# A decoder layer on one core: the last two output projections in front of context products 4 to 6, and the weight splits behind them

## What is computed

```
x = layernorm(x + attn(x))            # 32 heads of 32, then @ attn_ow + attn_ob
q1 = (clip(round(x / s1 + z1), 0, 255) - z1) * s1
q2 = (clip(round(ctx / s2 + z2), 0, 255) - z2) * s2      # ctx: 2 x 1024 x 1024
x = layernorm(x + q1 @ q2)
logits = x @ W_router.T               # 8 experts, the best two weighted
hw = (x @ A.T) * combine              # 8 experts of rank 16
x = layernorm(x + x @ W_base.T + b_base + hw @ B * 2)
```

## Time and profile before

| | before |
|---|---|
| median of 3 runs | 758.9 us (757.3 to 759.88) |
| profiled execution, time | 757.49 us |
| profiled execution, span | 755.7 us |
| PE busy | 720.2 us, 95% |
| DVE busy | 461.1 us, 61% |
| ACT busy | 427.0 us, 57% |
| POOL busy | 246.6 us, 33% |
| mean granted TensorE clock | 0.981 |

### The profile page before, as it was taken

How to read it: one execution, slowest core, us unless ns; L and a number is a source line. 1 busy time by engine, 2 the same in 40 slices (tenths; PEclk the granted TensorE clock), 3 DMA queues, 4 the chain that set the end, 5 groups by cost and what they waited for, 6 DMA issues and landing times.

```text
span 755.7 us, 11772 instructions
## 1 busy us (share of the span) xinstructions
PE 720.2 (95%) x3512; PEld 535.6 (71%) x3512; DVE 461.1 (61%) x831; ACT 427.0 (57%) x919; POOL 246.6 (33%) x189
## 2 busy tenths in 40 slices
PE   7989999999999999999999997996999987999996
PEld 5767768668668668668668664664766755888884
DVE  5867557557557567467567463416564699666564
ACT  5458668668668668668668576524555564221111
POOL 6260330240240240240140176636535275031111
PEclk9999999999999999999999997998999998999999
DMA  9665436436435435435433646526642153113101
GB/s 298 193 169 180 113 85 194 111 85 195 109 90 188 110 89 188 112 88 189 111 88 109 175 135 216 174 71 197 221 139 85 62 190 112 57 58 110 56 29 56
DMA packets 56020, 98.97 MB, mean 131 GB/s; under 512 B 11184, under 2 KB 21680, under 8 KB 55088
## 3 DMA queue, kind: packets, MB, share of 16 engines
q1 hardware_dynamic: 55696, 98.13, 42.4%
q10 hardware_dynamic: 288, 0.39, 0.2%
HBM read 56.41 MB, written 16.65 MB: 97 GB/s over the span
## 4 chain that ended last, share of the span: by engine, by line
PE 71%; issue 13%; DVE 5%; POOL 5%; DMA 2%; ACT 2%; SPq 2%; POOLq 0%; DVEq 0%; ACTq 0%
PE bank L451 43%; PE bank L574 8%; PE bank L588 8%; PE bank L544 7%; PE bank L699 2%; POOL xb L1158 2%; SPq L236 2%; PE bank L502 1%; POOL mv L1137 1%; DVE st L1415 1%; POOL big_lo L1150 1%; DMA cx_raw<-ctx_scratch 1%; ACT quant L901 0%; ACT x1s L897 0%; DMA xres<-in_x 0%
## 5 line engine op out<-in xcount | busy, mean ns | idle before, releaser
L840 ACT ACTIVATE probs<-bank 128x512 f32<-128x512 f32 x256 | 153.1, 598 | 134.2 <-PE bank L574 131.6
L1336 DVE TENSOR_REDUCE m_col<-bank 128x1 f32<-128x512 f32 x256 | 172.7, 687 | 86.8 <-PE bank L544 86.2
L845 ACT ACTIVATE bank<-bank,m_col 128x512 f32<-128x512 f32 x256 | 169.5, 662 | 14.1 <-DVE m_col L1336 13.2
L451 PE MATMUL bank<-big_hi,w_hi 128*128 128x512 f32 x384 | 157.4, 410 | 5.5 <-DVE big_lo L1233 5.5
L451 PE MATMUL bank<-big_lo,w_hi 128*128 128x512 f32 x384 | 153.0, 399 | 0.0
L451 PE MATMUL bank<-big_hi,w_lo 128*128 128x512 f32 x384 | 151.6, 395 | 0.0
L574 PE MATMUL bank<-qp,kp 98*128 98x512 f32 x256 | 102.9, 402 | 2.2 <-DMA qp<-m_row 2.2
L544 PE MATMUL bank<-kp,qp 96*128 96x512 f32 x256 | 102.7, 401 | 2.0 <-ACT bank L845 2.0
L1087 POOL TENSOR_SCALAR c_raw<-c_raw,sc 128x1024 f32<-128x1024 f32 x16 | 19.3, 1204 | 255.8 <-DMA c_raw<-in_ctx 250.9
L451 PEld LDWEIGHTS bank<-big_hi,w_hi 128*128 128x128 f32 x384 | 73.4, 191 | 24.9 <-DVE big_lo L1233 6.0
L451 PEld LDWEIGHTS bank<-big_hi,w_lo 128*128 128x128 f32 x384 | 73.1, 190 | 17.2
(11 more groups left out here) (140 smaller groups left out, 1021.5 us busy)
## 6 DMA issues: line engine op xcount, KB each, us to landing
w_raw<-in_wqkv SPq DMA_DIRECT2D x7, 1536.0 KB, 7.0
c_raw<-in_ctx SPq DMA_DIRECT2D x16, 512.0 KB, 4.0
qp<-q_hi SPq DMA_DIRECT2D x128, 64.0 KB, 2.0
kp<-k_hi SPq DMA_DIRECT2D x124, 64.0 KB, 2.0
big_raw<-in_xT SPq DMA_DIRECT2D x16, 256.0 KB, 5.4
qp<-q_lo SPq DMA_DIRECT2D x64, 64.0 KB, 2.0
c_scratch<-c_q SPq DMA_DIRECT2D x16, 256.0 KB, 2.2
r_all<-r_scratch SPq DMA_DIRECT2D x64, 64.0 KB, 2.0
```

Of the source, the lines that this page charges most:

```text
L451: mm = nc.tensor.matmul(dst, lhs[a], rhs[b], start=(k == 0 and n == 0) if first is None else False, stop=(k == last_k and n == 2))
L840: nc.scalar.activation(probs[:, j, t, :], bank(ST0 + i % 2), ACT.Exp).then_inc(sem["exp_ok"], 1)
L845: nc.scalar.activation(bank(MAX[n % 3]), bank(MAX[n % 3]), ACT.Exp, bias=m_col[:, n:n + 1], accum_out=l_col[:, 1 - par, n:n + 1]).then_inc ...
L1336: nc.vector.reduce_max(m_col[:, n:n + 1], bank(MAX[n % 3]), AX, negate=True).then_inc(sem["rowmax"], 1)
```

## The change

On TensorE both halves of tile 7's output projection come directly behind tile 6's; after them `transpose_c1(5)`, product 4, `transpose_c1(6)`, `transpose_x2(0)`, product 5, `hidden(0)`, product 6. The other engines' lists follow: rounding and splits of base half 0 stand directly behind tile 6's quantisation, and product 4's work behind them. On GpSimd both corrections and both bias sums move back, on SP the store of x2 tile 4 moves behind the loads of base half 1. The instructions are the same in number and shape.

```diff
@@ sync
             sp.dma_start(bb_sb[:, :], bb.rearrange("(a n) -> a n", a=1).to_broadcast([P, H])).then_inc(sem["bt_in"], 16)
-            store_x2(4)
             sp.wait_ge(sem["cx_split"], NT // 2)
...
                 sp.dma_start(big_raw[:, k, S:2 * S], wbT[k * P:(k + 1) * P, S:2 * S]).then_inc(big_in[1][k], 16)
+            store_x2(4)
             store_x2(5)
@@ tensor
             for n in (6, 7):
                 for h in range(2):
                     out_project(n, h)
-                transpose_c1(n - 1)
-                context_product(n - 2)
+            transpose_c1(5)
+            context_product(4)
+            transpose_c1(6)
             transpose_x2(0, 0, 0)
+            context_product(5)
+            hidden(0)
             context_product(6)
-            hidden(0)
             last_step(0, 0, 0, True)
@@ scalar
             normalise_x2(3)
-            copy_c1T(5)
-            scale_product(4)
             normalise_x1(6)
-            centre_c1(6)
-            normalise_x2(4)
             for k in range(KT):
                 round_wb(0, k)
+            copy_c1T(5)
+            centre_c1(6)
+            scale_product(4)
             copy_c1T(6)
-            scale_product(5)
             copy_x2T(0, first_x2_banks)
             normalise_x1(7)
+            scale_product(5)
+            centre_c1(7)
+            normalise_x2(4)
+            exp_logits(0)
             scale_product(6)
-            exp_logits(0)
-            centre_c1(7)
-            for k in range(4):
-                round_wb(1, k)
             normalise_x2(5)
-            for k in range(4, KT):
+            for k in range(KT):
                 round_wb(1, k)
             normalise_x2(6)
@@ gpsimd
             rstd1(6)
-            add_correction(6)
-            rstd2(4)
             for k in range(1, KT, 2):
                 split_wb(0, k)
             rstd1(7)
+            add_correction(6)
+            rstd2(4)
+            add_correction(7)
+            rstd2(5)
+            for k in range(1, KT, 2):
+                split_wb(1, k)
+            rstd2(6)
             pool.wait_ge(sem["bt_in"], 32)
             add_bias(0, 0, 0)
-            rstd2(5)
-            add_correction(7)
-            split_wb(1, 1)
-            split_wb(1, 3)
-            rstd2(6)
-            split_wb(1, 5)
-            split_wb(1, 7)
             add_bias(1, 1, 0)
@@ vector
             first_mean(6)
-            add_product(4)
-            row_correction(5)
             quantise(6)
-            product_stats(4)
-            second_mean(4)
             for k in range(0, KT, 2):
                 split_wb(0, k)
             residual_sum(7)
+            first_mean(7)
+            add_product(4)
+            row_correction(5)
+            split_x2T(0, 0)
+            quantise(7)
+            product_stats(4)
+            second_mean(4)
             add_product(5)
             row_correction(6)
-            first_mean(7)
-            split_x2T(0, 0)
+            route(0)
             product_stats(5)
-            quantise(7)
             second_mean(5)
-            route(0)
+            split_wb(1, 0)
+            split_wb(1, 2)
             add_product(6)
             row_correction(7)
-            split_wb(1, 0)
-            split_wb(1, 2)
-            product_stats(6)
             split_wb(1, 4)
             split_wb(1, 6)
+            product_stats(6)
             second_mean(6)
```

## The result

The change takes 765.07 us (median of 4 runs, 764.28 to 766.52) against 758.1 us of the kernel before (4 runs, 757.0 to 759.88): ratio 1.0092, 95% interval 1.0065 to 1.0119. The forecast was 766.1 us, in a range from 758.5 to 769.5. A second set of 4 runs of the same kernel, given further down, came out at 766.96 us, ratio 1.0123.

What follows compares the result with a forecast made beforehand. VectorE's chain up to the split of the transposed expert weights, as late as TensorE's, was taken to decide; +6.0 + 1.7 - 0.5 = +7.2 us gave a median of 766.1 us, range 762 to 769.5 (758.5 to 769.5 with variants).

Steps and rivals of the forecast that it cites:

- Front part and SP's queue: TensorE up to the first base half: 2.4 us ahead; the late x2 store costs 0.7 us, nothing in the sum.
- Middle: VectorE's chain to the second base half's split: TensorE starts that half 1.8 us earlier, after waiting 4.2 us.
- Back part, +6.0: VectorE before the split of hw: bias sums on GpSimd hold bt_hi and bt_lo; split comes 6.0 us later.
- the difference of two counts, 5.7: Split of hw: forward count of the new order against the same count over the old order, 5.7 us later.
- the plain count of 7.3: VectorE's chain counted forward to the split of hw, 644.55 against 637.23 in the trace of before: 7.3 us late.
- the count of the old order: The same forward count over the old order, to the split of hw: 638.8, 1.6 us later than the trace.
- Clock, +1.7: TensorE after its 8 us wait for the split of hw: half clock costs 1.7 us, bounds 0 and 2.6.
- hw(1), -0.5: TensorE's wait of 0.5 us for hw(1) goes, since VectorE has that 0.5 by then: -0.5 us.
- Sum: Whole kernel: +6.0 + 1.7 - 0.5 = +7.2 us, median 766.1 us.
- The faster rival: TensorE's new density pays as VectorE's chain reaches the hw split before the second base half ends: 755 us, chance 0.10.
- The same: Rival: bias sums do not hold up the bt pair, so 4.7 us go: +2.5, 761.4 us, chance 0.12.
- The signs named for a wrong forecast: transpose_c1(7) starting before 638 us, or bt_lo done before the second add_bias.

Runs made afterwards that it cites:

- The first experiment: The change, with GpSimd waiting for bt_ok so both bias sums come behind the bt pair: 762.04 us, ratio to the kernel before 1.0052.
- four strips ahead: The change, with ScalarE rounding four strips of the second weight half in front of normalise_x2(5) instead of behind it: 765.21 us, ratio 1.0082.
- the filler experiment: The change, with 28 matmuls nobody reads added on TensorE behind the second base half of tile 0: 764.75 us, ratio 1.0096.
- the combination of all moves: The change's TensorE order, with strips, weight splits, the bt pair and scale_product(7) moved on the other engines: 758.2 us, ratio to the kernel before 0.9994.
- bt off VectorE: The combination of all moves, with bt_hi on ScalarE, bt_lo on GpSimd, and copy_x2T(1) and two VectorE splits moved ahead: 755.71 us, ratio 0.9969.
- its variant with a late sum: The kernel before, with add_bias(0) moved to just in front of add_bias(1), all else in the old order: 759.22 us, ratio 1.0015.

## Why the prediction was right

The count on VectorE can be laid beside the trace step by step, in us from the mark (the prediction counted from 590.6):

| step | counted | measured |
|---|---|---|
| VectorE's splits of the first half end | 13.0 | 13.2 |
| product 4's matmuls end on TensorE | 14.8 | 14.8 |
| add_product(4) ends | 20.1 | 20.3 |
| first base half starts on TensorE | 25.5 | 25.6 |
| add_product(5) ends | 28.9 | 29.0 |
| routing ends | 31.9 | 32.0 |
| second base half starts on TensorE | 36.8 | 37.1 |
| bt_lo ends | 53.4 | 52.9 |
| split of hw ends | 53.95 | 53.4 |

- **Front part and SP's queue.** Right. TensorE has two waits of 0.3 us in place of 0.76 and 2.14; `transpose_x2(1)` starts 31.7 us from the mark, as counted for the late store, and the 0.7 us disappear in the wait behind it.
- **Middle.** Right: the wait in front of the second base half is 4.23 us (4.2 counted). What I left out is that this wait too is followed by low clock: eight matmuls from 626.13 took 3.46 us in place of 1.8. It costs nothing, since TensorE waits for VectorE afterwards.
- **Back part, +6.0.** It measured +6.54. The first experiment shows the meeting of the sums with the bt pair as the cause of 4.05 of them, where 4.7 were counted; the other 2.5 come from what stands ahead on VectorE's list, and four strips ahead took back 2.1 us. The size was set a little low: I took a value near the difference of two counts, 5.7, where the truth lies between it and the plain count of 7.3. The plain count came within 0.5 us of the place; the count of the old order is what erred.
- **Clock, +1.7.** It measured 1.99, 2.12 in the second execution of the change, and 1.9 in the filler experiment. The clock was at half until some 4.3 us after the restart in place of 3.4, since it was still at 0.50 in 644:646 and at 0.81 in 646:648.
- **hw(1), -0.5.** This term was a misreading. The row has one wait of 0.5 us somewhere behind 640 us, and it is not that of hw(1) but that of tile 7's hw, near the end. It is still there in the change. First the kernel before, then the change, from TensorE's timelines:

```profile
741.83 0.33 PE L752 MATMUL bank<-ident,hw 128*128 128x128 f32 x1 [0.53 <-DVE hw L1512]
748.66 0.33 PE L752 MATMUL bank<-ident,hw 128*128 128x128 f32 x1 [0.52 <-DVE hw L1510]
```

  Before, `transpose_hw` of tile 1 starts 1.07 us behind the start of `transpose_x2(2)`, in the change 0.87: there were 0.2 us to gain at hw(1), most of the 0.28 that came out.
- **Sum.** +7.2 forecast, +8.25 from the mark (6.54 + 1.99 - 0.28), +6.8 by the spans of the two profiled executions, +7.0 by the medians, and +8.8 by those of the second set. All three terms were off to the same side, 1.05 us together. That 766.1 still lies so near 765.07 is luck: the part ahead of the mark moves by 2 us between two executions of one kernel.

The faster rival needed VectorE to be 9 us ahead of the count; it is 0.5 ahead. *The same* is out by the change's own rows, where the bt pair takes 2.70 and 3.24 us beside the sums. Its price for them, 4.7 us, was near the 4.05 that the first experiment took off; but with the sums out of bt's way the end is 4.9 us behind before, not 2.5, since the rest of the delay was larger than forecast and the sums and the clock take their toll one step later. The signs named for a wrong forecast did not appear: `transpose_c1(7)` starts at 642.49, and `bt_lo` ends at 641.90, behind both sums.

What my later expectations got wrong is worth as much. They treated the split of hw(0) as the only gate. Behind it ScalarE's copies of x2T and c1T come late as well, and the same sums, moved, hold x2T of tile 1 and through it hw(1). And in the combination of all moves I added up gains of single experiments, which overlap, where VectorE's filled time should have been counted.

## What to carry to other kernels

Denser work on the busiest engine was worth nothing here until the engine that feeds it arrived earlier too: count that engine's list forward to the instruction that gates the next part. When long two-input instructions of GpSimd are moved, look at what VectorE does at that very moment, and then at what it does one step later; the cost depends on the neighbour: one sum moved back cost 1.55 us at the end in the old order, and two sums beside the bt pair cost 3.4 in the new one. For differences of 1 to 2 us in 760, compare traces from a common mark rather than whole times. And look up where a wait stands before it enters a sum: a total over a stretch does not say to which tile it belongs.

## What the runs showed of the hardware

- The length of a wait alone doesn't tell whether the clock falls behind it. Behind 3.25 us all the matmuls ran at full clock (four strips ahead), behind 1.94 us (bt off VectorE) the clock fell after two and a half matmuls, and the same wait of 2.67 us was followed by 5.3 us of low clock in the kernel before and by about 3.4 in its variant with a late sum. In the kernel with the sums behind bt it fell after 1.4 us of work. Even two executions of the change differ: behind the same wait of 4.23 us the first matmul is already slow in one (0.67 us), and in the other the first takes 0.50 and only the third 0.63. What decides it is not settled here.
- The turns reach the smallest instructions. In the kernel before, this cast of two columns ends with GpSimd's `add_correction` (621.23 to 623.63 us); in the next tile, without one beside it, it takes 0.17 us. VectorE's timeline of the kernel before:

```profile
622.01 1.64 DVE L1494 CAST rt<-ridx 128x2 f32<-128x2 uint32 x1
```

- The part ahead of the mark, the same work in the same order, ended between 588.99 and 594.10 us. Most of the difference lies before 507 us, in the attention; no run here shows why.
